# TensorE's expert program written out with the expert number loaded a tile ahead, and a reordered scan step

## The reference, cut to what matters

```
# state space scan, 64 heads of 8 values, state of 64, 2 sequences of 2048
dt  = softplus(dt_raw + dt_bias);  a = exp(-exp(A_log) * dt)
phi = cumsum(dt)[..., None] * rope_freqs           # rotates B and C, for every head
h_t = a_t * h_{t-1} + u_t (x) B_t                  # per head
y_t = h_t . C_t
...
# mixture of experts: 8 experts, 2 a token, hidden 224
scores = softmax(x @ gate_w);  sel = top_k(scores + bias, 2)
h   = silu(routed @ w1[e]) * (routed @ w3[e]);  routed_out = h @ w2[e]
```

## Time and profile before

| | us |
|---|---|
| median of three runs | 2707.72 |
| profiled execution, its own time | 2706.93 |
| its span, first to last instruction | 2704.9 |
| VectorE's last scan step ends, about | 1498 |
| experts, weight loads of `up`, first to last | 1890.2 to 2161.1 |

### The profile page before, as it was taken

The page is one execution under the profiler, slowest core; times in us unless marked ns, Lnnn a source line. Parts: engine busy times, 40 slices in busy tenths (PEclk is TensorE's granted clock), DMA queues, the critical chain, the costliest instruction groups (busy, mean ns, idle before and its releaser), DMA issues. The chain is left out here.

```text
span 2704.9 us, 61578 instructions
## 1 busy us (share of the span) xinstructions
PE 2159.2 (80%) x19761; PEld 1584.5 (59%) x19762; DVE 1936.6 (72%) x5279; ACT 1540.5 (57%) x3098; POOL 1486.3 (55%) x2287
## 2 busy tenths in 40 slices
PE   8947888888888878888887799784888847758887
PEld 5625555555565555565555688563444435548887
DVE  4539999999999999999999344465222257747776
ACT  5658888998999888888895122453111112212222
POOL 2437777887788777777787133342111144415444
PEclk9977888898888898888897899787999978879999
DMA  5766666665666666656664476343122233321110
GB/s 173 239 200 167 164 167 164 167 186 156 175 172 167 167 167 165 175 158 159 167 179 120 130 234 202 127 136 108 66 70 68 63 92 116 115 79 44 47 43 31
DMA packets 295365, 373.44 MB, mean 138 GB/s; under 512 B 44852, under 2 KB 234870, under 8 KB 295126
## 3 DMA queue, kind: packets, MB, share of 16 engines
q1 hardware_dynamic: 285254, 343.10, 45.5%
q0 software_dynamic: 9872, 27.28, 3.0%
HBM read 151.03 MB, written 85.00 MB: 87 GB/s over the span
## 5 line engine op out<-in xcount | busy, mean ns | idle before, releaser
L667 POOL TENSOR_TENSOR p_CR<-p_pc 128x256 f32<-128x256 f32 x512 | 373.4, 729 | 218.2 <-DVE p_pc L986 195.9
L671 POOL TENSOR_TENSOR p_BR<-p_pb 128x256 f32<-128x256 f32 x512 | 373.3, 729 | 26.0
L999 DVE TENSOR_TENSOR p_M<-p_ps_sc,p_D 128x512 f32<-128x512 f32 x512 | 327.3, 680 | 71.6 <-PE p_ps_sc L748 71.6
L748 PE MATMUL p_ps_sc<-p_CR,p_BR 64*128 64x128 f32 x4096 | 321.7, 300 | 69.0 <-DVE p_M L999 47.7
L748 PEld LDWEIGHTS p_ps_sc<-p_CR,p_BR 64*128 64x128 f32 x4096 | 272.5, 201 | 129.4 <-issue 101.1
L881 ACT ACTIVATE p_D<-p_ps_x 128x512 f32<-128x512 f32 x512 | 275.4, 589 | 80.5 <-PE p_ps_x L714 78.9
L763 PE MATMUL p_ps_y<-p_M,p_uexp 128*32 128x128 f32 x4096 | 290.8, 295 | 3.3 <-issue 2.3
L986 DVE SCALAR_TENSOR_TENSOR p_pc<-p_ps_c,p_beta,p_cs 128x256 f32<-128x256 f32 x512 | 243.1, 475 | 31.2 <-DMA p_sn<-p_tr_s 28.4
L763 PEld LDWEIGHTS p_ps_y<-p_M,p_uexp 128*32 128x32 f32 x4096 | 228.0, 118 | 46.0 <-issue 31.8
L986 DVE SCALAR_TENSOR_TENSOR p_pc<-p_ps_c,p_beta,p_sn 128x256 f32<-128x256 f32 x512 | 242.7, 474 | 0.0
L992 DVE SCALAR_TENSOR_TENSOR p_pb<-p_ps_b,p_beta,p_cs 128x256 f32<-128x256 f32 x512 | 242.6, 474 | 0.0
(11 more groups left out here) (278 smaller groups left out, 5417.1 us busy)
## 6 DMA issues: line engine op xcount, KB each, us to landing
p_cs<-p_tr_c SPq DMA_DIRECT2D x256, 256.0 KB, 4.0
p_sn<-p_tr_s SPq DMA_DIRECT2D x256, 256.0 KB, 4.5
p_phib<-scratch_phi SPq DMA_DIRECT2D x256, 128.0 KB, 3.1
p_x<-scratch_rt SPq DMA_DIRECT2D x72, 128.0 KB, 2.0
scratch_ro<-p_o POOLq DMA_DIRECT2D x72, 128.0 KB, 2.0
p_xT<-in_xT SPq DMA_DIRECT2D x64, 128.0 KB, 4.4
scratch_u<-p_u SPq DMA_DIRECT2D x16, 512.0 KB, 3.6
scratch_wu<-p_wu SPq DMA_DIRECT2D x16, 512.0 KB, 4.3
```

The source lines that it names most:

```text
L667: e.tensor_tensor(CR[:, p, g, :], pc[:, g % 2, 0, :], pc[:, g % 2, 1, :], ALU.add).then_inc(S["rotC"], 1)
L671: e.tensor_tensor(BR[:, p, g, :], pb[:, g % 2, 0, :], pb[:, g % 2, 1, :], ALU.add).then_inc(S["rotB"], 1)
L748: m = e.matmul(sc_ps[half][:, (g * 2 + b) * L:(g * 2 + b + 1) * L], BR[half * 64:half * 64 + 64, p, 2 * q + g, b * L:(b + 1) * L], CR[half ...
L999: e.tensor_tensor(M[:, m_slot(p, n), :], sc_ps[n % 2][:, :], D[:, n, :], ALU.mult).then_inc(S["m_ok"], 1)
```

## The change

In the scan TensorE issues `scores(t, p, 3)` and the exponents of the next step ahead of the first `outputs`. ScalarE's `turns` are split again into their two parts and spread between the decays; the fourth quarter goes to the end of the step and one step further ahead; `held_bc` moves behind `decays` 6 and 7. In the experts TensorE's loop is unrolled over all 72 tiles, and the expert number is loaded once a tile, right behind `up` of the tile before, at a constant address, and kept for `down`.

```diff
@@ TensorE's scan step
-                outputs(t, k, 0, 0)
                 scores(t, p, 3)
                 if more:
                     exponents(t + 1, 1 - p, 0)
+                outputs(t, k, 0, 0)
                 outputs(t, k, 0, 1)
@@ ScalarE's scan step
                 decays(t, 2)
+                if ahead:
+                    in_turns(t + 3, (k + 3) % NB, 0)
                 decays(t, 3)
-                if soon:
-                    turns(t + 2, (k + 2) % NB, 3)
+                if ahead:
+                    whole_turns(t + 3, (k + 3) % NB, 0)
                 if t and t <= LAST:
                     turned(t - 1, 2)
                     turned(t - 1, 3)
                 if ahead:
-                    turns(t + 3, (k + 3) % NB, 0)
+                    in_turns(t + 3, (k + 3) % NB, 1)
                 decays(t, 4)
                 decays(t, 5)
                 if ahead:
-                    turns(t + 3, (k + 3) % NB, 1)
+                    whole_turns(t + 3, (k + 3) % NB, 1)
+                if t + 2 < T:
+                    magnitude(t + 2, p, 0)
+                decays(t, 6)
+                if ahead:
+                    in_turns(t + 3, (k + 3) % NB, 2)
+                decays(t, 7)
                 if k == NB - 1 and t + 1 < T:
                     held_bc(c + 1)
-                if soon:
-                    magnitude(t + 2, p, 0)
-                decays(t, 6)
-                decays(t, 7)
+                if ahead:
+                    whole_turns(t + 3, (k + 3) % NB, 2)
                 if 2 <= t < LAST + 2:
                     state(t - 2)
                 if t < LAST:
                     turned(t, 0)
-                if ahead:
-                    turns(t + 3, (k + 3) % NB, 2)
                 ...
                 if t < LAST:
                     turned(t, 1)
+                if ahead:
+                    in_turns(t + 3, (k + 3) % NB, 3)
+                    whole_turns(t + 3, (k + 3) % NB, 3)
@@ TensorE's program of the experts
             def expert(j):
-                return e.value_load(tab[0:1, bass.ds(j + NTILE, 1)], min_val=0, max_val=NE)
+                return e.value_load(tab[0:1, NTILE + j:NTILE + j + 1], min_val=0, max_val=NE)
...
-            def step(j, i, last=False):
-                p = i % 2
-                if not (isinstance(j, int) and j == 0):
-                    turn_h(j - 1, 1 - p)
-                up(j, p)
-                if not last:
-                    turn_x(j + 1, (i + 1) % NX)
-                if not (isinstance(j, int) and j == 0):
-                    down(j - 1, 1 - p)
-            turn_x(0, 0)
-            for i in range(NX):
-                step(i, i)
-            with e.Fori(1, NTILE // NX - 1) as j:
-                for i in range(NX):
-                    step(j * NX + i, i)
-            for i in range(NX):
-                step(NTILE - NX + i, i, i == NX - 1)
+            turn_x(0, 0)
+            before, now = None, expert(0)
+            for j in range(NTILE):
+                p = j % 2
+                if j:
+                    turn_h(j - 1, 1 - p)
+                up(j, p, now)
+                if j < NTILE - 1:
+                    after = expert(j + 1)
+                    turn_x(j + 1, (j + 1) % NX)
+                if j:
+                    down(j - 1, 1 - p, before)
+                before, now = now, after
             turn_h(NTILE - 1, 1)
-            down(NTILE - 1, 1)
+            down(NTILE - 1, 1, before)
```

More of the change, by code:

```diff
@@ L890, in step @@
                 p = k % 2
-                ahead, soon = t + 3 < T, t + 2 < T
+                ahead = t + 3 < T
                 decays(t, 2)
+                if ahead:
+                    in_turns(t + 3, (k + 3) % NB, 0)
                 decays(t, 3)
-                if soon:
-                    turns(t + 2, (k + 2) % NB, 3)
+                if ahead:
+                    whole_turns(t + 3, (k + 3) % NB, 0)
                 if t and t <= LAST:
@@ L937, in state, with all_turns @@
                                  ).then_inc(S["x_ok" if h else "kept"], 1)
-            def turns(s, k, u):
-                in_turns(s, k, u)
-                whole_turns(s, k, u)
+            def all_turns(s):
+                for u in range(NQ):
+                    in_turns(s, s, u)
+                    whole_turns(s, s, u)
             for s in range(2):
-                for u in range(NQ):
-                    turns(s, s, u)
+                all_turns(s)
                 if s == 0:
@@ L952, in _ @@
                 decays(0, n)
-            for u in range(NQ - 1):
-                turns(2, 2, u)
+            all_turns(2)
             for k in range(NB):
@@ L1843, in turn_x, with up @@
                 m.then_inc(S["xt_mm"], 1)
-            def up(j, p):
-                x = expert(j)
+            def up(j, p, x):
                 at_least(e, S["xt_ok"], j, 1, 1)
@@ L1859, in turn_h, with down @@
                 m.then_inc(S["ht_mm"], 1)
-            def down(j, p):
-                x = expert(j)
+            def down(j, p, x):
                 at_least(e, S["ht_ok"], j, 1, 1)
```

## The result

The changed kernel takes 2640.8 us, the median of four runs (2630.04 to 2651.93), against 2707.41 for the kernel before. The ratio is 0.975, with a 95% interval of 0.970 to 0.980: about 67 us faster. That is in the predicted range of 2594 to 2666, 22 us above the forecast of 2619 and 3 us outside the range of 2603 to 2638 that the forecast gave itself. The profiled execution took 2641.73, span 2639.7.

The account below looks back on a forecast made before the run. VectorE was taken to bound the scan, ScalarE 5% behind; in the experts TensorE's sequencer idled before `up`. Experts 47 plus scan 42 is 89 us off 2706.93, 2617.9, put at 2619 against the median; range 2594 to 2666.

Parts of the forecast that it names:

- Experts, 47 us: Experts, TensorE: without the load between `turn_h` and `up`, gap 0.40 us, period 3.80 to 3.14, gain 47 us.
- The cover of the load: Experts: behind `up`, the load's 0.67 us hides in the 1.24 us before `turn_x` starts, so costs nothing.
- TensorE's scan order, 38 to 56 us: Scan: `scores(t, p, 3)` ahead of the first `outputs` shortens VectorE's 39 score waits, by 38 to 56 us.
- the low price: Scan, TensorE at 2.4 GHz: each of 39 score waits loses at most 1.00 us, 38 us together.
- ScalarE's order: Scan: same ScalarE work reordered, in three moves that matter: 10 us gained, up to 13 lost, one counted even.
- (a): Scan, chunk ends: `held_bc` behind `decays` 6 and 7 lets `state` start early, about 10 us off the large waits.
- (b): Scan: late `held_bc` copies stall VectorE's first product by 0.9 us at 15 chunk ends, up to 13 us lost.
- (c): Scan, ScalarE: fourth quarter of turns delays `decays` 2 by about 1.2 us; `whole_turns` fills state-transpose waits; counted even.
- rival 1: Scan gains nothing net, 20 us at most, as ScalarE cannot give more: 2651, between 2641 and 2661; chance 0.20.
- Rival 2: Scan comes down to VectorE's own work, gaining 75 us: 2586; chance 0.11.
- Rival 3: Scan slower: late BT copies make `decayed` 4 wait and ScalarE's chain paces every step, +78 us: 2739; chance 0.04.
- Rival 4: Experts gain 14 instead of 47 us: load holds back `turn_x`, or written-out tiles starve on instruction fetch: 2652; chance 0.10.

Follow-up runs that it names:

- the square: Four kernels with TensorE's orders as changed: `held_bc` early or late with turns as before (2623.85, 2593.76 us), early or late with turns as changed (2656.82, 2637.12).
- `after_again`: The changed kernel itself, run again beside the other three of the square: 2637.12 us, ratio 0.972 to the kernel before.
- `held_late`: The changed kernel with ScalarE's turns in the order of before; `held_bc` stays behind `decays` 7: 2593.76 us, ratio 0.957 to the kernel before.
- `fourth_last`: `held_late` with the fourth quarter of the turns moved to the end of the step, for step t + 3: 2618.16 us, ratio 0.965.
- `turns_only`: The kernel before with only ScalarE's order of the scan changed: 2725.04 us, ratio 1.007.
- `turns_late`: The changed kernel with `held_bc` put back ahead of the magnitude and `decays` 6: 2656.82 us, ratio 0.980 to the kernel before.

## Why the prediction was right and where not

**Experts, 47 us: right in mechanism and size.** 47 us by the medians (2705.88 to 2659.03), 42 by the ratio, 45 by the periods. The gap was put at 0.40 and is 0.41. That the next limit is the xT copy was shown by moving it. The low end, 14 us for writing out alone, is 12.6 in the profile. The cover of the load is wider than reckoned: two loads fit.

**TensorE's scan order, 38 to 56 us: right, at the low price.** 37 us alone by the medians, 45 in the profile. The reasoning that the small waits vanish and the large ones shrink by 1.85 shows in the score waits from 300 to 1400 us: 61.9 us in 33, up to 3.8, become 14.6 in 13, up to 1.7. As reckoned, all of them were before `decayed` 6.

**ScalarE's order, (a) + 10, (b) - 13, (c) even: the step that failed.** The scan was put at 42 and gave 20 by the medians (67 less 47), 24 in the profiles. (b) was seen and sized rightly in sum: 10.9 us of such waits between 300 and 1400, though in 8 places of 1.4 on average. But it was charged to the wrong move. Behind `decays` 7, `held_bc` is worth 20 to 30 us; with the turns as before the stall is 0.9 us, so it needs a ScalarE that is late already, and what makes it late is (c). (a), put at 10, was too small at least with the turns as before, because it left out ScalarE's own wait at the early place. (c), "I count these even", is worth +33 to +43 us by the square. This is the term that failed. The working compared sums of idle time: the 0.9 us of state waits that `whole_turns` filled were slack on an engine 5% off the bound, and the delay of `decays` 2 was real. It is on the loop of ScalarE and TensorE over the two alternating banks: TensorE waits 42.5 us for `decays` 2 where it waited 0.2. From there the lateness reaches VectorE in three ways, as `after_again` beside `held_late` shows: score waits of 20.1 us, the stall for the copies (11.9 after 0.9) and sine waits (10.8 after 4.6). Which of them comes depends on the rest of the order, since in `fourth_last` it is hardly the scores. That the loop is the way is read from these waits, and a part of the loss may go by way of TensorE's clock; no run tells the two apart.

**The choice of 42 and the hit.** The bounds worked out were 35 and 53, and the low price was the measured one. The sum at that price, 35, would have given 2626, 15 us below the measured time, so not even the lower bound reaches it. That the result lies in the range of 2594 to 2666 is owed to the room left for rival 1. And it is in part luck that the forecast misses by 22 only, because two errors nearly cancel: (c), put at nothing, costs 33 to 43 us, and the place of `held_bc`, put at a loss of 3, gains 20 to 30.

**Its own signs.** "Issue" before `up`, the period (3.17) and the 72 loads are as said for right. The scan is on the edge: score waits 28.9 us where under 25 was said, a mean step of 19.6 at the end of 19.0 to 19.6, the stalls for the copies as said. None of the signs of being wrong came: 0.2 us of waits for D, sine waits of 9.6, a clock of 0.89.

**Rivals.** Rival 1 (waits change their name) describes the scan best. Its upper end, a scan gain of 20 and 2641, is the measured result; it was given 0.20, the forecast 0.55. Rival 2, VectorE's floor, was given 0.11 "against: (b)". It is reachable, with the turns left alone: `held_late` is at 2594, and 2586 was its number. Rival 3's mechanism is real, its price too high. In `turns_only` VectorE does wait before `decayed` 4, 34 times, but for 8.5 us in all beside 38.2 before `decayed` 6, and the order is 19 us slower by itself, not 78. Rival 4 did not happen in either form: 72 tiles written out show no "issue" time before `up`'s matmuls, in agreement with the section "Instruction fetch mechanics" of "Runtime: NRT & Kernel Launch" of the Trainium skill, which has straight code streamed ahead.

## What to carry to other kernels

When one engine is the bound and another is a few per cent behind, moving work of that second engine into its idle places can cost more than it fills: here +33 to +43 us. Ask instead which instruction of it starts a chain back to the bound, and be slow to put anything before that one; here one such instruction was `decays` 2. A rare long item (here 1.5 us once in four steps) belonged behind the instructions that others wait for, although its own consumer then sometimes waits (-20 to -30 us). A register load that the sequencer must wait for cost 0.47 us a tile where it stood between `turn_h` and `up`, and nothing, even twice, behind `up`, where the transposes that follow are not due for another 1.24 us. And a change of three edits is to be run as three.

## What was not expected of the hardware

The same written-out scan program gave executions 18 us apart in y to y (1248.7 to 1266.6). Within one kernel the faster executions show the higher granted clock: the kernel before, in the last group, ran at 2696.18 with 0.892 and at 2722.75 with 0.878. Between kernels this holds only roughly. Of the profiles here the scan with 0.95 is the one at VectorE's floor, but the one with the lowest clock, 0.82, is that of `turns_late`, whose y to y of 1259.6 is that of the kernel before at 0.87. Its stretch from 300 to 1400 us:

```profile
300.00:1400.00 1100.00, 958.69 (x12432) 679.23 (x12426) 1033.69 (x2394) 980.69 (x1901) 874.12 (x1524) 0.82 0.64 167
```

Whether the clock makes the time or the waits make the clock, no run here separates.
